# A ViT block on one core: order of VectorE's work in a step, order of SyncE's loads, and who stores the last rows

## Chip, cores and metric

The kernel runs on one core of one Trainium2 chip. The metric is the device time of one execution in microseconds, as the median of several runs. The engines are called PE (TensorE), PEld (its weight loads), ACT (ScalarE), DVE (VectorE), POOL (GpSimd) and SP (SyncE, which here only issues DMAs).

## What is computed

```python
# x (128,224,224,3) f32: an image and four cropped copies of it, in patches of 16x16
h = tokens(x) @ W + b                     # (128, 196, 192), W folded over the five copies
h = concat([cls_tok, h], axis=1)          # (128, 197, 192)
n = (h - mean(h)) / sqrt(var(h) + 1e-5)
q, k, v = n @ Wq.T, n @ Wk.T, n @ Wv.T    # 6 heads of 32
s = q k^T * 32**-0.5 + lam * anchor_sim   # per head
h = h + (softmax(s) @ v) @ Wo.T
n = layernorm(h)
i = clip(round(n / 0.02), -128, 127)      # int8
h = h + (i @ weight_t) * 0.0002 + bias
```

## The kernel before

There are two blocks of code, one after the other, each with a program for every engine, and a barrier between them.

**The token block** (`build_tokens`) holds all 128 images on the partitions and works through the 14 rows of 14 patches. DVE transposes pixels, PE multiplies by the folded weights, DVE adds the bias and takes the statistics (`bn_stats`), POOL forms the factors (`norm_factors`, nine small links, each waiting for the one before) and normalises. `h` and the normalised `xn` go to scratch tensors in HBM by POOL's DMA queue. Of the last row POOL normalises only the first `EARLY` = 8 of 14 tokens in this block and stores them (line 590). The other six follow in the next block: POOL forms their factors, DVE normalises them (line 1183), SP stores them (line 767). Meanwhile POOL sets a row of ones in `k_st` (line 1230), for which PE waits before its first image.

**The image block** (`build_attention`) is a software pipeline over the images. In step `i`, f = image i+5 is transposed (its `x_hi` and `x_lo` parts are made), pair p is projected to q and k, a = i+1 gets its scores and their maxima, b = i is scored again transposed and exponentiated (heads 0 to 4), c = i-1 is attended, e = i-2 gets output projection and h1, g = i-3 is normalised and quantised, k = i-4 goes through the last product and is stored. Steps alternate: in an odd step PE projects two blocks of a pair, in an even step the third. The first 12 images and the last 8 are written out, those between run in a loop of six steps. The order in each engine is written out by hand.

fp32 operands are split in a high part (made by ACT) and a low part (DVE: `x_lo`, `qk_lo`, `a_lo`), and PE multiplies the parts.

What matters here, engine by engine, in one step:
- PE: score 0 and 1; projection (line 803, it waits for `x_lo` of the step before); score_t 5 of c; in odd steps a second projection; score 2; last product; attend; score_t 0; score 3; output projection; score_t 1; turn back; transposes of `xn_in`; score 4; score_t 2; transposes of `qx` (wait for quantise); transposes of `att` (wait for DVE's product, line 1140); score 5; score_t 3; values; score_t 4; transposes of the maxima's parts.
- DVE: maxima 0 and 1; `qk_lo`; maximum 2; y; maximum 3; quantise of g (lines 1118 and 1121, waits for POOL); h1 of e (line 1129); reciprocal and `att` of c; maxima 4 and 5; the maxima's two parts (1150, 1152); `x_lo` of f (1160); `a_lo` of c (1168); statistics of e (1173).
- POOL: h1 plus bias (1198), wait for the statistics, nine links (139 to 147), `qx` (1216).
- SP: DMA issues for the q_st and k_st copies of a pair (707), the output (749, 750), the load of `xn_in` (714, 715: image i+6, two buffers), of `h_in` (756), and the maxima's rows into `q_st` (761).

Score h (h from 2) waits for maximum h-2, as two banks take turns.

Of the kernel before, what the change touches and what calls it, by code (L numbers as in the profile page):

```python
# [14 lines left out]
B, IMG, CH = 128, 224, 3  # L15
# [3 lines left out]
D = 192  # L19
# [130 lines left out]
def build_tokens(nc, s):  # L150
# [61 lines left out]
    h_stored = [sem(f"h_stored{i}") for i in range(2)]  # L212
    xn_stored = sem("xn_stored")

    SMALL = 16 * 5
# [53 lines left out]
    with nc.Block() as block:  # L269
        @block.sync  # L270
        def _(sp):
            def load(dst, src, landed):
                sp.dma_start(dst, src).then_inc(landed, 16)

            for g, landed in ((1, left_landed), (2, left_landed), (3, right_landed), (4, right_landed), (0, whole_landed)):
                load(w_of[g], s["tok_w"][:, RAW_ORDER.index(g)], landed)
            load_half_row(sp, 0, (0, 1), x_half[0])
            load(tok_bias[:], s["tok_b"].rearrange("(o n) -> o n", o=1).broadcast_to([B, D]), biases_landed)
            load_half_row(sp, 1, (0, 1), x_half[1])
            for i, w in enumerate(("wq", "wk", "wv")):  # L280
# [12 lines left out]

            rows(sp, step)
            sp.wait_ge(biases_landed, 32)

        @block.tensor
# [226 lines left out]
        def _(pool):  # L524
# [33 lines left out]
            def step(t):  # L558
# [28 lines left out]
                if first:  # L587
                    pool.dma_start(h_dram[:, 0, :], h_t[:, 0, G, :]).then_inc(cls_landed, 16)
                    pool.dma_start(xn_dram[:, 0, :], xn_t[:, G, :]).then_inc(xn_stored, 16)
                pool.dma_start(xn_dram[:, bass.ds(at_token, T), :] if last else xn_dram[:, bass.ds(at_token, G), :],  # L590
                               xn_t[:, 0:T if last else G, :]).then_inc(xn_stored, 16)

            rows(pool, step)

    return pads_stored, cls_landed, h_stored, xn_stored


def build_attention(nc, s):
# [7 lines left out]
    h_t, xn_t, stats, ln, o_bank = (s[n] for n in ("h_t", "xn_t", "stats", "ln", "o_bank"))  # L606
    pads_stored, cls_landed, h_stored, xn_stored = s["tokens_stored"]
    NS, NP = 2, 3
    MOD = 2 * NP
# [7 lines left out]
    def tile(name, shape, dt=F32):  # L617
        return sb(name, shape, dt, attention)

    xn_in = tile("xn_in", [TC, NS, 2, DA + 2 * DB])  # L620

# [81 lines left out]
    with nc.Block() as block:  # L703
        @block.sync
        def _(sp):
# [4 lines left out]
            def load_xn(n):  # L710
                if n.reuses(NS):
                    sp.wait_ge(xt_done, n.count(1, 1 - NS))
                by_chunk = xn_dram[n.n].rearrange("(c p) d -> p c d", p=TC)
                sp.dma_start(xn_in[:, n.two, :, 0:D], by_chunk).then_inc(xn_landed[n.slot], 16)
                sp.dma_start(xn_in[:, n.two, :, D:DA + 2 * DB], by_chunk[:, :, DA:D]).then_inc(xn_landed[n.slot], 16)

            def step(i):
                f, p, a, c, k, ahead = i.plus(5), pair_of(i), i.plus(1), i.plus(-1), i.plus(-4), i.plus(6)
                if i.fixed and i.n == -5:
                    load_xn(f)  # L720
                if p.within(B) and i.r % 2:
                    q_first, q_last, k_first = (0, 4), (4, H), (0, SPLIT)
# [24 lines left out]
                if k.within(B):  # L747
                    sp.wait_ge(y_done, k.count(1, 1))
                    sp.dma_start(out[k.n, 0:TC, :], y[:, k.two, 0, :]).then_inc(y_stored[k.slot], 16)
                    sp.dma_start(out[k.n, TC:NTOK, :], y[0:NTOK - TC, k.two, 1, :]).then_inc(y_stored[k.slot], 16)  # L750
                if ahead.within(B):
                    load_xn(ahead)
                if c.within(B):
# [17 lines left out]
            for p in range(2):  # L771
                sp.wait_ge(h_stored[p], 16 * (G // 2 - p))
            sp.wait_ge(xn_stored, 16 * (G + 1))
            images(sp, step)
# [4 lines left out]
        def _(pe):  # L779
            def turn(bank, src, n, width):  # L780

                for ic in range(2):
                    for c in range(2):
                        last = pe.transpose(bank[0:width, ic * TP + c * TC:ic * TP + (c + 1) * TC],  # L784
                                            src[:, n.two, c, ic * width:(ic + 1) * width], ident[0:TC, 0:TC])
                return last
# [90 lines left out]
            def step(i):  # L877
# [68 lines left out]
                if has_f:  # L946
# [7 lines left out]
                    turn(MISC[2], xn_in, f, DA).then_inc(xt_done, 1)  # L954
                if has_a:
# [3 lines left out]
                if has_g:  # L959
                    pe.wait_ge(quant_done, g.count(2, 2))  # L960
                    if has_e:
                        pe.wait_ge(h1_done, e.count(1, 1))
                    elif has_k:
                        pe.wait_ge(qxt_done, k.count(1, 1))
                    turn(MISC[0], qx, g, DC).then_inc(qt_done, 1)
                if has_c:

                    pe.wait_ge(norm_done, c.count(1, 1))
                    turn(o_bank[:, 0, :], att, c, DC).then_inc(at_done, 1)
                if has_a:  # L970
# [102 lines left out]
        def _(dve):  # L1073
# [15 lines left out]
            def step(i):  # L1089
# [15 lines left out]
                if has_k:  # L1105
                    dve.wait_ge(ff_done, k.count(1, 1))
                    dve.wait_ge(hb_done, k.count(1, 1))
                    if k.reuses(NS):
# [4 lines left out]
                        .then_inc(y_done, 1)  # L1113
                if has_a:
                    maxima(a, 3)
                if has_g:
# [4 lines left out]
                    nc.vector.tensor_scalar(qx[:, g.two, :, :], qx[:, g.two, :, :], MAGIC + 127.0, MAGIC - 128.0,  # L1121
                                            ALU.min, ALU.max).then_inc(quant_done, 1)
                if has_e:

# [18 lines left out]
                if has_a:  # L1143
# [4 lines left out]
                    if a.reuses(NS):  # L1148
# [4 lines left out]
                                            max_parts[:, a.two, :, 0:H].bitcast(F32),  # L1153
                                            ALU.subtract).then_inc(mpart_done, 1)
                if has_f:
                    dve.wait_ge(xhi_done, f.count(1, 1))
# [7 lines left out]
                if has_c:  # L1164
                    dve.wait_ge(ahi_done, c.count(1, 1))
                    if c.reuses(NS):
                        dve.wait_ge(op_done, c.count(1, 1 - NS))
                    nc.vector.tensor_tensor(a_lo[:, c.two, :, :], wide(o_bank[:, 0, :], DC),
                                            a_hi[:, c.two, :, :].bitcast(F32), ALU.subtract).then_inc(alo_done, 1)
                if has_e:  # L1170
                    dve.wait_ge(h1_done, e.count(1, 1))
                    for cc in range(2):
                        last = nc.vector.bn_stats(st2[:, e.two, cc, :], h1[:, e.two, cc, :])  # L1173
                    last.then_inc(st2_done, 1)

# [14 lines left out]
        def _(pool):  # L1190
# [32 lines left out]
            def link_last(ins):  # L1223
# [4 lines left out]
            norm_factors(nc, link_last, stats[:, LAST, EARLY:G, :], [ln[:, LAST, i, EARLY:G] for i in range(8)],  # L1228
                         minus_half[:, 0:G - EARLY])
            pool.memset(k_st[ST:ST + 2, :, :, :, :].bitcast(F32), 1.0).then_inc(ones_made, 1)  # L1230
            images(pool, step)
# [39 lines left out]
```

## Time and profile before

Three runs took 1878.80, 1881.69 and 1881.96 us, median 1881.69. The profiled execution took 1878.63 us, of which 1876.9 us are the span of the trace.

| | PE | PEld | DVE | ACT | POOL |
|---|---|---|---|---|---|
| busy us | 1752.2 | 1597.9 | 1413.3 | 781.9 | 740.3 |
| share of the span | 93% | 85% | 75% | 42% | 39% |

The token block lasts until 432 us, the pipeline of images is full from about 512 us. TensorE's granted clock is at its full level in all but the slices around the start of either block and the last one. Matmuls are pipelined, so the time that one takes is best read as the distance from its start to the start of the next.

### The profile page before, as it was taken

The numbers are of one execution on the slowest core, as the hardware profiler recorded it, in microseconds if no ns is written. First come the engines' busy times: TensorE is split into PE (matmuls) and PEld (weight loads), VectorE is DVE, ScalarE is ACT, GpSimd is POOL, SyncE is SP. The second block draws the span as 40 slices with busy tenths as digits, with TensorE's granted clock in tenths as the row PEclk, the third lists the DMA queues.
The fourth block names the chain that finished last, engine by engine and source line by source line (L and its number), as shares of the span: only waits on it lengthen the run. The fifth ranks groups of instructions, "written<-read, shape, count | busy, mean of one in ns | idle before, by whom it ended". The sixth has DMA issues, their size and how long they took to land.

```text
span 1876.9 us, 51604 instructions
## 1 busy us (share of the span) xinstructions
PE 1752.2 (93%) x15344; PEld 1597.9 (85%) x15344; DVE 1413.3 (75%) x3646; ACT 781.9 (42%) x1878; POOL 740.3 (39%) x1910
## 2 busy tenths in 40 slices
PE   1999999992799999999999999999999999999995
PEld 1999999992688888888888888888888888888884
DVE  4888888883477777777777777777777777777773
ACT  2000000000355555555555555555555555555552
POOL 3343453452044343443434434344343443434434
PEclk8999999996899999999999999999999999999997
DMA  9789999954777777787777777778777787777751
GB/s 281 215 277 303 310 316 280 310 211 108 112 129 137 140 134 134 129 134 139 134 135 128 134 139 134 135 128 134 139 134 135 128 133 138 135 136 127 135 99 30
DMA packets 214779, 303.57 MB, mean 162 GB/s; under 512 B 47584, under 2 KB 203635, under 8 KB 204612
## 3 DMA queue, kind: packets, MB, share of 16 engines
q1 hardware_dynamic: 204542, 227.27, 64.0%
q10 hardware_dynamic: 6054, 38.54, 7.2%
q0 software_dynamic: 4128, 37.06, 5.1%
q8 instruction: 30, 0.49, 0.1%
q14 instruction: 25, 0.20, 0.0%
HBM read 126.49 MB, written 58.29 MB: 98 GB/s over the span
## 4 chain that ended last, share of the span: by engine, by line
issue 30%; POOL 23%; PE 9%; DVE 8%; POOLq 3%; DMA 1%; SPq 1%; ACT 0%; DVEq 0%; ACTq 0%
POOL hb L1198 6%; POOL ln L146 4%; POOL qx L1216 4%; DVE h L1129 3%; DVE qx L1118 2%; PE o_bank L863 2%; PE bank L803 2%; POOLq L1208 2%; POOL ln L139 1%; POOL ln L145 1%; POOL ln L143 1%; POOL ln L147 1%; POOL ln L144 1%; POOL ln L141 1%; POOL ln L142 1%
## 5 line engine op out<-in xcount | busy, mean ns | idle before, releaser
L1078 DVE TENSOR_REDUCE neg_max<-bank 99x2 f32<-99x394 f32 x768 | 419.9, 560 | 243.7 <-PE bank L835 242.5
L1005 ACT ACTIVATE probs<-bank 99x396 f32<-99x396 f32 x768 | 383.5, 499 | 278.6 <-PE bank L847 278.4
L317 PE MATMUL bank<-e_t,xt 128*128 128x192 f32 x2352 | 388.3, 329 | 39.0 <-DVE xt L403 22.4
L317 PEld LDWEIGHTS bank<-e_t,xt 128*128 128x128 f32 x2352 | 386.8, 192 | 40.3 <-DVE xt L403 23.5
L847 PE MATMUL bank<-q_st,k_st 98*99 98x198 f32 x1536 | 284.5, 267 | 11.2 <-DMA q_st<-max_rows 6.1
L863 PE MATMUL o_bank<-probs,vals 99*64 99x198 f32 (+1 forms) x3072 | 290.3, 337 | 0.4 <-issue 0.3
L835 PE MATMUL bank<-k_st,q_st 96*99 96x198 f32 x1536 | 275.1, 274 | 7.5 <-issue 3.3
L863 PEld LDWEIGHTS o_bank<-probs,vals 99*64 99x64 f32 (+1 forms) x3072 | 213.0, 137 | 48.6 <-issue 1.1
L847 PEld LDWEIGHTS bank<-q_st,k_st 98*99 98x99 f32 x1536 | 202.5, 166 | 59.0 <-issue 36.5
L403 DVE STREAM_TRANSPOSE xt<-x_t 128x256 f32<-128x256 f32 x588 | 214.9, 416 | 44.7 <-PE bank L317 44.2
L999 ACT ACTIVATE x_hi<-bank 128x396 fp32r<-128x396 f32 x128 | 63.3, 495 | 414.2 <-PE bank L784 414.2
L1198 POOL TENSOR_TENSOR hb<-h,ffn_bias 99x384 f32<-99x384 f32 x128 | 128.3, 1003 | 244.8 <-DVE h L1129 244.8
L835 PEld LDWEIGHTS bank<-k_st,q_st 96*99 96x99 f32 x1536 | 192.5, 167 | 28.4 <-DVE neg_max L1078 13.9
L999 ACT ACTIVATE o_t<-o_bank 97x396 f32<-97x396 f32 (+1 forms) x256 | 93.1, 416 | 294.5 <-PE o_bank L863 294.5
L139 POOL TENSOR_TENSOR ln<-st 99x2 f32<-99x2 f32 x128 | 25.3, 198 | 405.7 <-DVE st L1173 405.7
L1216 POOL TENSOR_SCALAR qx<-h,ln 99x192 f32<-99x192 f32 x256 | 127.4, 505 | 41.0 <-POOL ln L147 41.0
L146 POOL TENSOR_TENSOR ln<-ln,minus_half 99x2 f32<-99x2 f32 (+2 forms) x143 | 127.5, 892 | 25.4 <-POOL ln L145 25.3
L1086 DVE TENSOR_TENSOR qk_lo<-bank,qk_hi 128x396 fp32r<-128x396 f32 x192 | 108.6, 565 | 30.8 <-ACT qk_hi L1012 27.0
L824 PE MATMUL bank<-wo_lo,a_hi 96*99 96x192 f32 x512 | 128.9, 252 | 0.0
L823 PE MATMUL bank<-wo_hi,a_hi 96*99 96x192 f32 x512 | 128.8, 252 | 0.0
L825 PE MATMUL bank<-wo_hi,a_lo 96*99 96x192 f32 x512 | 128.7, 251 | 0.0
L1012 ACT ACTIVATE qk_hi<-bank 128x396 fp32r<-128x396 f32 x192 | 96.3, 502 | 50.3 <-PE bank L803 42.3
(121 smaller groups left out, 3340.3 us busy)
## 6 DMA issues: line engine op xcount, KB each, us to landing
x_t<-in_x_dram ACTq DMA_DIRECT2D x26, 1344.0 KB, 18.3
x_t<-in_x_dram SPq DMA_DIRECT2D x26, 1344.0 KB, 22.1
q_st<-qk_hi SPq DMA_DIRECT2D x128, 198.0 KB, 4.2
k_st<-qk_hi SPq DMA_DIRECT2D x128, 198.0 KB, 4.7
xn_in<-xn_scratch SPq DMA_DIRECT2D x128, 148.5 KB
h_in<-h_scratch SPq DMA_DIRECT2D x128, 148.5 KB
h_scratch<-h_t POOLq DMA_DIRECT2D x13, 1344.0 KB, 17.6
xn_scratch<-xn_t POOLq DMA_DIRECT2D x13, 1344.0 KB, 8.2
```

Of the source, the lines that this page charges most:

```text
L146: link(nc.gpsimd.tensor_tensor(v[6], v[4], half, ALU.pow))
L317: last = pe.matmul(token_bank(p)[:, 0:D], xt[:, p, c // 3, c % 3, :], e_t[:, row_kind(t), col, c // 3, c % 3, :], start=c == 0, stop=c == 5)
L403: last = nc.vector.transpose(xt[:, p, :, c, :].rearrange("p m (g b) -> p g m b", b=32), pix[:, c])
L824: pe.matmul(acc, hi, wo_lo[:, ic, :], start=False, stop=False)
L835: last = pe.matmul(S_BANK[h % 2][0:TC, c * TP:(c + 1) * TP], q_st[0:ST, n.pair, h, n.two, c * TC:(c + 1) * TC], k_st[0:ST, n.pair, h, n.tw ...
L847: last = pe.matmul(T_BANK[0:TC, c * TP:(c + 1) * TP], k_st[:, n.pair, h, n.two, c * TC:(c + 1) * TC], q_st[:, n.pair, h, n.two, :], start= ...
L863: last = pe.matmul(o_bank[half * TW:(half + 1) * TW, p // 2, (p % 2) * TP:(p % 2 + 1) * TP], vals[0:kk, n.two, kc, h, :], probs[0:kk, n.tw ...
L999: nc.scalar.activation(dst, src, ACT.Copy, **affine).then_inc(done, 1)
L1005: nc.scalar.activation(probs[:, n.two, h, :, :], wide(T_BANK, TC), ACT.Exp).then_inc(exp_done, 1)
L1078: nc.vector.tensor_reduce(out=neg_max[:, n.two, :, h], in_=wide(S_BANK[h % 2], TC)[:, :, 0:NTOK], axis=AX_X, op=ALU.max, negate=True).then ...
L1198: nc.gpsimd.tensor_tensor(hb[:, e.two, :, :], h1[:, e.two, :, :], ffn_bias[:].unsqueeze(1).broadcast_to([TC, 2, D]), ALU.add).then_inc(hb_ ...
L1216: nc.gpsimd.tensor_scalar(qx[:, e.two, cc, :], h1[:, e.two, cc, :], v[7][:, cc:cc + 1], v[6][:, cc:cc + 1], ALU.add, ALU.mult).then_inc(ln ...
```

## The change

- SP stores the first eight tokens of the last row, behind a wait for POOL's normalisation, with a semaphore of its own; POOL no longer does.
- POOL's memset of ones in `k_st` waits for DVE's six normalisations.
- `xn_in` has three buffers instead of two. SP loads image i+7 at the head of its step, ahead of the copies of q and k; before, it was image i+6, behind the output.
- DVE quantises g before maximum 3 and not behind it.
- DVE takes the statistics of e right behind the maxima's parts, and then `x_lo` and `a_lo`.

```diff
+            at_token = (G - 1) * G + 1                      # SP, end of the token block
+            sp.wait_ge(ln_step, G * LN_PER)
+            sp.dma_start(xn_dram[:, at_token:at_token + EARLY, :], xn_t[:, 0:EARLY, :]).then_inc(early_stored, 16)
...
-                pool.dma_start(xn_dram[:, bass.ds(at_token, T), :] if last else xn_dram[:, bass.ds(at_token, G), :],
-                               xn_t[:, 0:T if last else G, :]).then_inc(xn_stored, 16)
+                if not last:
+                    pool.dma_start(xn_dram[:, bass.ds(at_token, G), :], xn_t[:, 0:G, :]).then_inc(xn_stored, 16)
...
-    xn_in = tile("xn_in", [TC, NS, 2, DA + 2 * DB])
+    xn_in = tile("xn_in", [TC, NX, 2, DA + 2 * DB])         # NX = 3
...
-                if n.reuses(NS):
-                    sp.wait_ge(xt_done, n.count(1, 1 - NS))
+                if n.reuses(NX):
+                    sp.wait_ge(xt_done, n.count(1, 1 - NX))
...
-                f, p, a, c, k, ahead = i.plus(5), pair_of(i), i.plus(1), i.plus(-1), i.plus(-4), i.plus(6)
+                f, p, a, c, k, ahead = i.plus(5), pair_of(i), i.plus(1), i.plus(-1), i.plus(-4), i.plus(7)
                 if i.fixed and i.n == -5:
                     load_xn(f)
+                    load_xn(f.plus(1))
+                if ahead.within(B):
+                    load_xn(ahead)
...
-                if ahead.within(B):                         # behind the output's stores
-                    load_xn(ahead)
...
-            sp.wait_ge(xn_stored, 16 * (G + 1))
+            sp.wait_ge(xn_stored, 16 * G)
+            sp.wait_ge(early_stored, 16)
...
-                if has_a:                                   # DVE
-                    maxima(a, 3)
                 if has_g:
                     dve.wait_ge(ln2_step, g.count(LN2_PER, LN2_PER))
...
+                if has_a:
+                    maxima(a, 3)
                 if has_e:
...
+                if has_e:                                   # DVE, behind the maxima's parts
+                    dve.wait_ge(h1_done, e.count(1, 1))
+                    for cc in range(2):
+                        last = nc.vector.bn_stats(st2[:, e.two, cc, :], h1[:, e.two, cc, :])
+                    last.then_inc(st2_done, 1)
                 if has_f:                                   # x_lo; then a_lo
...
-                if has_e:                                   # the same four lines, behind a_lo
...
+            pool.wait_ge(last_row_xn, G - EARLY)
             pool.memset(k_st[ST:ST + 2, :, :, :, :].bitcast(F32), 1.0).then_inc(ones_made, 1)
```

## Rows read from the trace of the kernel before

**Rows 1.** Waits: engine, line, tile, releaser; us in total, times, longest.
```profile
POOL ln L139 <- DVE st L1173: 405.7, 127, 3.3
SPq L761 <- ACT max_rows L999: 325.4, 123, 8.0
```
**Rows 2.** Time line of PE in the loop: start us, us, engine, line, operands, count.
```profile
1003.01 0.35 PE L847 MATMUL bank<-q_st,k_st 98*99 98x198 f32 x2
...
1004.21 0.38 PE L784 MATMUL o_bank<-ident,att 99*96 99x99 f32 x2 [0.22 <-DVE att L1140]
...
1014.42 0.35 PE L847 MATMUL bank<-q_st,k_st 98*99 98x198 f32 x2
...
1014.97 0.38 PE L784 MATMUL o_bank<-ident,att 99*96 99x99 f32 x2
...
1018.59 0.34 PE L803 MATMUL bank<-x_lo,wb_rest 97*128 97x396 f32 x1
1018.87 0.34 PE L835 MATMUL bank<-k_st,q_st 96*99 96x198 f32 x1
...
1024.49 0.35 PE L847 MATMUL bank<-q_st,k_st 98*99 98x198 f32 x2
...
1025.53 0.38 PE L784 MATMUL o_bank<-ident,att 99*96 99x99 f32 x2
```
**Rows 3.** Time line of DVE in the same steps.
```profile
1005.96 0.63 DVE L1160 TENSOR_TENSOR x_lo<-bank,x_hi 128x198 fp32r<-128x198 f32 x2
...
1016.72 0.63 DVE L1160 TENSOR_TENSOR x_lo<-bank,x_hi 128x198 fp32r<-128x198 f32 x2
...
1017.74 0.60 DVE L1173 BATCH_NORM_STATS2 st<-h 99x6 f32<-99x192 f32 x2
1018.27 0.54 DVE L1078 TENSOR_REDUCE neg_max<-bank 99x2 f32<-99x394 f32 x1
...
1023.52 0.36 DVE L1118 TENSOR_SCALAR qx<-qx 99x384 f32<-99x384 f32 x1 [0.57 <-POOL qx L1216]
...
1024.19 0.55 DVE L1129 TENSOR_TENSOR h<-bank,h_in 99x384 f32<-99x384 f32 x1
...
1059.25 0.63 DVE L1160 TENSOR_TENSOR x_lo<-bank,x_hi 128x198 fp32r<-128x198 f32 x2
```
**Rows 4.** Time line of PE's weight loads, first load of a projection.
```profile
1006.70 0.19 PEld L803 LDWEIGHTS bank<-x_hi,wa_hi 128*128 128x128 f32 x1
...
1017.75 0.19 PEld L803 LDWEIGHTS bank<-x_hi,wa_hi 128*128 128x128 f32 x1
...
1060.42 0.19 PEld L803 LDWEIGHTS bank<-x_hi,wa_hi 128*128 128x128 f32 x1
```
**Rows 5.** Chain that ended last, image block's start: start us, us, what.
```profile
449.48 0.91 PE bank L784 x4
...
483.49 0.53 SPq L714
...
484.54 4.43 DMA q_st<-max_rows
```
**Rows 6.** Drains of lines 269 and 703 (ends of blocks): ns min/median/max, first/last start.
```profile
L269 POOLq DRAIN  x1: 5038/5038/5038, 427.1 to 427.1; - x1
L269 DVEq DRAIN  x1: 399/399/399, 427.8 to 427.8; - x1
...
L703 POOLq DRAIN  x1: 1074/1074/1074, 1869.6 to 1869.6; - x1
```
**Rows 7.** Lines 1183 and 1230: ns min/median/max, first and last start us.
```profile
L1183 DVE TENSOR_SCALAR xn_t<-h_t,ln x6: 360/364/6173, 436.1 to 443.4; 128x192 f32<-128x192 f32 x6
...
L1230 POOL MEMSET k_st<- x1: 6032/6032/6032, 436.1 to 436.1; 2x7128 f32 x1
```
**Rows 8.** Time line of DVE near the end.
```profile
1855.25 0.56 DVE L1140 TENSOR_TENSOR att<-o_bank,inv_sum 99x384 f32<-99x384 f32 x1
...
1857.46 0.61 DVE L1173 BATCH_NORM_STATS2 st<-h 99x6 f32<-99x192 f32 x2
```

More of the change, by code:

```diff
@@ L213, in build_tokens @@
     xn_stored = sem("xn_stored")
+    early_stored = sem("early_stored")
     SMALL = 16 * 5
@@ L589, in step @@
                     pool.dma_start(xn_dram[:, 0, :], xn_t[:, G, :]).then_inc(xn_stored, 16)
-                pool.dma_start(xn_dram[:, bass.ds(at_token, T), :] if last else xn_dram[:, bass.ds(at_token, G), :],
-                               xn_t[:, 0:T if last else G, :]).then_inc(xn_stored, 16)
+                if not last:
+                    pool.dma_start(xn_dram[:, bass.ds(at_token, G), :], xn_t[:, 0:G, :]).then_inc(xn_stored, 16)
             rows(pool, step)
-    return pads_stored, cls_landed, h_stored, xn_stored
+    return pads_stored, cls_landed, h_stored, xn_stored, early_stored
 def build_attention(nc, s):
@@ L606, in build_attention @@
     h_t, xn_t, stats, ln, o_bank = (s[n] for n in ("h_t", "xn_t", "stats", "ln", "o_bank"))
-    pads_stored, cls_landed, h_stored, xn_stored = s["tokens_stored"]
-    NS, NP = 2, 3
+    pads_stored, cls_landed, h_stored, xn_stored, early_stored = s["tokens_stored"]
+    NS, NP, NX = 2, 3, 3
     MOD = 2 * NP
@@ L710, in load_xn @@
             def load_xn(n):
-                if n.reuses(NS):
-                    sp.wait_ge(xt_done, n.count(1, 1 - NS))
+                if n.reuses(NX):
+                    sp.wait_ge(xt_done, n.count(1, 1 - NX))
                 by_chunk = xn_dram[n.n].rearrange("(c p) d -> p c d", p=TC)
-                sp.dma_start(xn_in[:, n.two, :, 0:D], by_chunk).then_inc(xn_landed[n.slot], 16)
-                sp.dma_start(xn_in[:, n.two, :, D:DA + 2 * DB], by_chunk[:, :, DA:D]).then_inc(xn_landed[n.slot], 16)
+                sp.dma_start(xn_in[:, n.slot % NX, :, 0:D], by_chunk).then_inc(xn_landed[n.slot], 16)
+                sp.dma_start(xn_in[:, n.slot % NX, :, D:DA + 2 * DB], by_chunk[:, :, DA:D]).then_inc(xn_landed[n.slot], 16)
             def step(i):
-                f, p, a, c, k, ahead = i.plus(5), pair_of(i), i.plus(1), i.plus(-1), i.plus(-4), i.plus(6)
+                f, p, a, c, k, ahead = i.plus(5), pair_of(i), i.plus(1), i.plus(-1), i.plus(-4), i.plus(7)
                 if i.fixed and i.n == -5:
                     load_xn(f)
+                    load_xn(f.plus(1))
+                if ahead.within(B):
+                    load_xn(ahead)
                 if p.within(B) and i.r % 2:
@@ L779, in _, with turn @@
         def _(pe):
-            def turn(bank, src, n, width):
+            def turn(bank, src, at, width):
                 for ic in range(2):
@@ L784, in turn @@
                         last = pe.transpose(bank[0:width, ic * TP + c * TC:ic * TP + (c + 1) * TC],
-                                            src[:, n.two, c, ic * width:(ic + 1) * width], ident[0:TC, 0:TC])
+                                            src[:, at, c, ic * width:(ic + 1) * width], ident[0:TC, 0:TC])
                 return last
@@ L953, in step @@
                         pe.wait_ge(xlo_done, f.count(1, 0))
-                    turn(MISC[2], xn_in, f, DA).then_inc(xt_done, 1)
+                    turn(MISC[2], xn_in, f.slot % NX, DA).then_inc(xt_done, 1)
                 if has_a:
@@ L964, in step @@
                         pe.wait_ge(qxt_done, k.count(1, 1))
-                    turn(MISC[0], qx, g, DC).then_inc(qt_done, 1)
+                    turn(MISC[0], qx, g.two, DC).then_inc(qt_done, 1)
                 if has_c:
                     pe.wait_ge(norm_done, c.count(1, 1))
-                    turn(o_bank[:, 0, :], att, c, DC).then_inc(at_done, 1)
+                    turn(o_bank[:, 0, :], att, c.two, DC).then_inc(at_done, 1)
                 if has_a:
@@ L1169, in step @@
                                             a_hi[:, c.two, :, :].bitcast(F32), ALU.subtract).then_inc(alo_done, 1)
-                if has_e:
[L1171 to L1174, printed above, removed]
             nc.vector.memset(vals[:], 0.0).then_inc(consts, 1)
```

## The prediction

> **What bounds the kernel now.** I read the page of the profile first. TensorE (PE) is busy 93% of the span and VectorE (DVE) 75%, so the time is near a PE floor, and a DVE edit pays only where PE waits. Next the waits, sorted by total: GpSimd (POOL) stood 405.7 us for the statistics in 127 images, and SyncE (SP) 325.4 us for the maxima's rows [rows 1]. POOL is no bottleneck, so its wait costs nothing by itself; the question is who waits for what POOL makes. For that I read PE's own time line in the image loop. From the last product of score_t(b,2) to the transposes of `att` PE takes 0.55 us in an odd step (1014.42 to 1014.97), 1.04 in an even one (1024.49 to 1025.53) and 1.20 in every third even one (1003.01 to 1004.21), where the loop also jumps [rows 2]. So PE loses 0.49, 0.49 and 0.65 us in three pairs of images, 0.54 on average. DVE's time line says why: `quantise` began at 1023.52, released by POOL's qx, and h1, the reciprocal and `att` queue behind it [rows 3].
>
> This is a closed chain: statistics, POOL's nine links and qx, quantise, h1, att, PE's transposes, score 5, maxima 4 and 5, their parts, x_lo, a_lo, statistics again. It sets the pace of every step, so shortening it pays until PE's next wait.
>
> That next wait is the thing to look for. The weight load of the block projection (line 803) began at 1006.70, and x_lo, which it waits for, ran from 1005.96 for 0.63 us, to 1006.59: a hand-over of 0.11 us, hence already released by x_lo [rows 3, 4]. In an even step x_lo ended at 1017.35 and the load began at 1017.75, 0.40 later; in every third at 1059.88 and 1060.42, 0.54 later [rows 3, 4].
>
> **Part 1, statistics ahead of x_lo and a_lo.** In the old order x_lo began at 1016.72 and the statistics at 1017.74: they start 1.02 us sooner. The statistics occupy DVE for 0.53 us (1017.74 to 1018.27) [rows 3], and x_lo and a_lo come that much later. What it gives: POOL's qx is ready at 1022.50 instead of 1023.52. What it costs:
> - odd step: nothing covers x_lo, so the projection starts 0.53 us later.
> - even step: the cover is 0.40-0.11 = 0.29, so 0.24 is left; in every third 0.54-0.11 = 0.43, so 0.10.
> - given back: after the even projection, score 2 began 0.28 after the last product (1018.59 to 1018.87) because maximum 0 had begun only at 1018.27; its weight load is 0.19 long and sets the usual distance [rows 2 to 4]. A projection that starts later hides these 0.09, except in the third pair.
> a_lo is read only by the next step's attention, several us on: nothing, and if that cover were gone at most another 0.53.
>
> **Part 2, quantise ahead of maximum 3.** Quantise takes 0.67 (1023.52 to 1024.19), a maximum 0.48-0.57. New quantise: 1022.50 to 1023.17, then maximum 3 to 1023.65, then h1, 0.54 before its old 1024.19. PE's loss there was 0.49, so the whole loss goes, with 0.05 us in hand and 0.15 to 0.24 more from PE's own later projection. In odd steps the scores come 0.5 later too and quantise falls into DVE's idle time. Maximum 3 is later by up to 0.9 us, but only score 5 needs it, which comes after the transposes of `att`. The average per pair:
> two pairs of three: +0.53 +0.24 -0.09 -0.49 = +0.19; the third: +0.53 +0.10 -0.65 = -0.02; mean +0.12 us.
> 128 images are 64 pairs, less two at either end where the pipeline fills and empties: 60 such pairs, **+7.2 us**. The bounds: +0.02 a pair if the even delays were all hidden (0.53 against 0.54: 0 us), +0.24 if no score 2 wait is given back and 0.05 of the loss stays (14 us). I take 7.2, since each term is a start-to-start difference in a pattern that repeats to 0.02 us.
>
> **Part 3, token loads first in SP's step, third buffer.** The two loads take 1.05 us (483.49 to 484.54) [rows 5]. They stand before the maxima's rows in the same step and now fall into the time that SP spends waiting, 325.4 us in 123 steps, 2.6 a step [rows 1]. In the loop this is worth nothing: no PE wait there is on these loads. If that cover went, the q_st and k_st copies behind them would be up to 1.05 later, and they are used two steps on. At the start it is on the chain: PE waits for the first rows, issued at 484.54 and 4.43 us under way [rows 5]. They go out 1.05 sooner: **-1.0 us** (0 to -1.5). The third buffer lets image 3's load go early, but the first scores wait for the k_st copies, not for it: 0.
>
> **Part 4, the first stored rows by SP.** POOL's drain at the block's end lasted 5.04 us from 427.1, right behind its last store, to 432.2; DVE's ended at 427.8+0.4 = 428.2. At the kernel's end POOL's drain, with no store before it, took 1.07 us [rows 6]. So the drain waits for the store. With POOL's last store a whole row of tokens earlier, the barrier falls to DVE's end, 428.3: **-3.9 us**; were POOL's drain 5 us in any case, it would only start one store issue sooner, -0.6.
>
> **Part 5, POOL's ones behind the last rows.** Six normalisations of the last rows: 0.36 us each, but one took 6.17, and in exactly that time POOL's memset ran for 6.03, both from 436.1; the last began at 443.4, so the others follow at 0.3 [rows 7]. With the memset behind them the six take 5x0.29+0.36 = 1.8 instead of 7.6, and the rows are stored 5.8 us sooner. PE's first transposes, 449.48 before [rows 5], have them at 449.48-5.8 = 443.7. But now the memset starts at 436.1+1.8 = 437.9 and ends at 443.95, and PE waits for the ones: 444.05. So **-5.4 us** (from -6, if the memset overlaps all, to -4.2, if DVE's two memsets of x_lo, 1.2 us, had to queue behind it). I take the -5.4, since DVE's operations of the loop keep their 0.55 to 0.63 us beside POOL's links [rows 3], so it is not every operation that is shut out. The Trainium skill (SBUF — State Buffer, Who interferes with whom) says that GpSimd and a VectorE operation in a two-port mode exclude each other for the whole instruction; the trace agrees, 6.17 us against 0.36. By its rule DVE's memsets, with no SBUF input, would not queue either, and the term stays what it is.
>
> **The tail.** For the last image but one, the statistics stood behind a_lo, which waited for ScalarE: 1857.46, with `att` begun at 1855.25 and 0.56 long [rows 8]. They now follow `att`, some 0.5 behind its start: 1855.75, **-1.7 us** on the chain that ends the kernel. In the few steps just before there is no x_lo left: half a microsecond of a_lo leaves the chain and maximum 3 enters it with as much: 0.
>
> **Sum:** +7.2 -1.0 -3.9 -5.4 -1.7 = -4.8 us. Against the profiled execution, 1878.63 (span 1876.9), this gives 1873.8. That execution lies at the low end of the three runs (1878.80, 1881.69, 1881.96), so beside the median 1881.69 it is **1876.9 us**. The forecast's own range: steady part 0 to +14, barrier -0.6 to -3.9, ones -4.2 to -6, rows 0 to -1.5: 1869 to 1884.
>
> **Rivals.**
> - A: PE is not held by x_lo. Then the 0.54 a pair comes in full: 60x0.54 = 32 us and the 12 us of start and tail: 1837. For it: POOL's chain is the longest loop now. Against it: the 0.11 us hand-over of rows 3 and 4. Chance 0.08.
> - B, slower: quantise holds DVE for POOL and maximum 3 then stands in front of h1. It decides as soon as maximum 3 ends after 1023.70, that is, if qx is ready later than 1022.55. If the old loss stays whole, the pair costs 0.53+0.13 = 0.66 more, 60x0.66 = 40, less 12: 1909. For it: only 0.05 us in hand. Against: PE's scores are themselves later, which leaves 0.2. Chance 0.07.
> - C: the change does not do what it says at the start: the barrier stays with POOL, so -0.6 instead of -3.9, and the sum is -1.5: 1880. Against: the 1.07 us drain. Chance 0.13.
> - D, slower by a little: the steady part at its upper bound and the gains of the start at their lower ones: +14 -0.6 -4.2 -1.7 = +7.5: 1889. For it: the even steps' terms are small differences, and each 0.1 us a pair is 6 us. Chance 0.10.
> The forecast has 0.62.
>
> **How the numbers follow.** Range 1868 to 1887: it leaves out A, B and a part of D, some 0.2. What tells a change from none is 0.2%, 3.8 us: 1877.9 to 1885.5. Faster: A 0.08, some two thirds of the forecast's 0.62 (its value is only 1 us inside the bound), 0.03 of C: 0.51. Slower: B 0.07, most of D 0.07, 0.04 of the rest: 0.18. Same: 0.31.
>
> **What would show it.** Right: the load of line 803 in odd steps still 0.11 us behind x_lo, with the statistics ahead of it; score_t to `att` 0.55 us in every step; three steady pairs 0.3 to 0.4 us longer than before (one is 1004.21 to 1025.53 = 21.32 [rows 2]); no 5 us drain and the second block starting near 428.3; the six normalisations at 0.36 each; PE's first transposes near 440.1. Wrong: pairs near 20.8 (A) or 22 (B), a drain of 5 us (C), or DVE's memsets 6 us long.

## The result and the profile after

Four runs of the changed kernel took 1859.11 to 1861.66 us, median **1860.83 us**. Four runs of the kernel before beside them took 1878.28 to 1881.96, median 1880.24: ratio **0.9898 (0.9883 to 0.9912)**. The profiled execution took 1860.42 us, span 1858.7, against 1876.9 before: -18.2. The sum of the prediction was -4.8, beside the median 1876.9 us with a range of 1868 to 1887: the measured time lies below the range. The direction was right, the size was not. One run of one experiment (e9) took 2405.72 us at a mean granted clock of 0.67, where every other run here had 0.97 to 0.98, and is left out of e9's ratio.

To see where the time went, the span is divided at two starts of h1 (the DVE operation of line 1129 before, 1135 after), the first and the 121st, which the trace gives to 0.01 us. The 120 steps between them are 60 pairs, the steady part:

| | first h1 | 121st h1 | between, per pair | 121st h1 to the end |
|---|---|---|---|---|
| before | 512.50 | 1792.07 | 21.33 | 84.8 |
| changed | 501.60 | 1775.61 | 21.23 | 83.1 |
| difference | **-10.9** | | -0.09, in 60 pairs **-5.6** | **-1.7** |

The start and the tail were forecast at -10.3 (-3.9 -5.4 -1.0) and -1.7. The steady part was forecast at +7.2 and is -5.6: of the 13.4 us between forecast and measured span, 12.8 are here.

The token block, which is the same in both up to its last stores, ends at nearly the same time in these two profiles. POOL's last normalisations start at 422.62 before and 422.67 changed:

```profile
422.62 3.90 POOL L582 TENSOR_SCALAR xn_t<-h_t,ln 128x192 f32<-128x192 f32 x8 [0.31 <-POOL ln L147]
...
422.67 3.89 POOL L586 TENSOR_SCALAR xn_t<-h_t,ln 128x192 f32<-128x192 f32 x8 [0.31 <-POOL ln L147]
```

In other profiles this start lies between 421.13 (e1) and 423.82 (e9), and no edit reaches back before it. So a first h1 is compared by its distance from this start where tenths of a microsecond matter: 89.88 before, 78.93 changed.

The chain that ended last, from the page of the kernel before:

```profile
issue 30%; POOL 23%; PE 9%; DVE 8%; POOLq 3%; DMA 1%; SPq 1%; ACT 0%; DVEq 0%; ACTq 0%
```

and the page of the changed kernel, busy times and the same chain:

```profile
PE 1737.3 (93%) x15344; PEld 1602.8 (86%) x15344; DVE 1409.2 (76%) x3646; ACT 781.9 (42%) x1878; POOL 738.7 (40%) x1909
...
PE 62%; DVE 7%; issue 3%; POOL 2%; ACT 1%; SPq 1%; DMA 1%; DVEq 0%; POOLq 0%
```

PE now stands for 62% of the chain (9% before) and POOL for 2% (23%). So the chain no longer goes round through POOL's links. The waits of the changed kernel say the same (columns as in [rows 1]):

```profile
SPq L766 <- ACT max_rows L1005: 396.5, 127, 7.0
...
POOL ln L139 <- DVE st L1164: 277.4, 127, 2.3
...
DVE qx L1122 <- POOL qx L1222: 124.3, 128, 3.0
...
PE bank L809 <- DVE x_lo L1171: 25.7, 63, 1.3
```

POOL waits 277.4 us for the statistics and not 405.7 [rows 1]. And 63 projections of PE, one in each odd step, have `x_lo` named as what ended their wait; before, only two had. This is the next wait that the prediction looked for. The time line of PE (columns as in [rows 2]) has first the projection of an even step, then that of an odd one, then that of every third even step, and last the transposes of `att` in every third even step:

```profile
1002.92 0.41 PE L841 MATMUL bank<-k_st,q_st 96*99 96x198 f32 x2
...
1005.55 0.42 PE L809 MATMUL bank<-x_hi,wa_hi 128*128 128x396 f32 x1
...
1012.08 0.35 PE L853 MATMUL bank<-q_st,k_st 98*99 98x198 f32 x2
...
1012.62 0.55 PE L790 MATMUL o_bank<-ident,att 99*96 99x99 f32 x4
1012.95 0.41 PE L841 MATMUL bank<-k_st,q_st 96*99 96x198 f32 x2
...
1015.58 0.42 PE L809 MATMUL bank<-x_hi,wa_hi 128*128 128x396 f32 x1 [0.41 <-DVE x_lo L1171]
...
1045.29 0.41 PE L841 MATMUL bank<-k_st,q_st 96*99 96x198 f32 x2
...
1048.01 0.36 PE L809 MATMUL bank<-x_hi,wa_hi 128*128 128x396 f32 x1
...
1054.49 0.35 PE L853 MATMUL bank<-q_st,k_st 98*99 98x198 f32 x2
...
1055.13 0.55 PE L790 MATMUL o_bank<-ident,att 99*96 99x99 f32 x4
```

From score_t(b,2) to the transposes of `att` PE now takes 0.54 us in this even step (1012.08 to 1012.62), as in odd steps before [rows 2]: the loss of 0.49 is gone. In every third even step it takes 0.64 (1054.49 to 1055.13), so 0.10 of that loss stays. From score 5 to the projection it takes 2.63 in the even and the odd step (1002.92 to 1005.55, 1012.95 to 1015.58) and 2.72 in every third even one (1045.29 to 1048.01). The same two starts in the kernel before, odd step, even step and every third even one:

```profile
1004.54 0.41 PE L835 MATMUL bank<-k_st,q_st 96*99 96x198 f32 x2
...
1006.74 0.43 PE L803 MATMUL bank<-x_hi,wa_hi 128*128 128x396 f32 x1
...
1015.29 0.41 PE L835 MATMUL bank<-k_st,q_st 96*99 96x198 f32 x2
...
1017.84 0.36 PE L803 MATMUL bank<-x_hi,wa_hi 128*128 128x396 f32 x1
...
1057.83 0.41 PE L835 MATMUL bank<-k_st,q_st 96*99 96x198 f32 x2
...
1060.51 0.36 PE L803 MATMUL bank<-x_hi,wa_hi 128*128 128x396 f32 x1
```

That is 2.20, 2.55 and 2.68. So the projection is late by 0.43 in the odd step (forecast 0.53), by 0.08 in the even one (0.24) and by 0.04 in every third (0.10). DVE's time line shows why, changed kernel, from the second of the maxima's parts on:

```profile
1014.21 0.17 DVE L1158 TENSOR_TENSOR max_parts<-neg_max,max_parts 99x12 fp32r<-99x12 f32 x1
1014.29 0.61 DVE L1164 BATCH_NORM_STATS2 st<-h 99x6 f32<-99x192 f32 x2
1014.82 0.61 DVE L1171 TENSOR_TENSOR x_lo<-bank,x_hi 128x198 fp32r<-128x198 f32 x2
```

and of the kernel before, the last two of the same operations:

```profile
1005.79 0.17 DVE L1152 TENSOR_TENSOR max_parts<-neg_max,max_parts 99x12 fp32r<-99x12 f32 x1
1005.96 0.63 DVE L1160 TENSOR_TENSOR x_lo<-bank,x_hi 128x198 fp32r<-128x198 f32 x2
```

The statistics do occupy DVE for 0.53 (1014.29 to 1014.82). But they start 0.08 us after the parts' subtraction (1014.21), where `x_lo` used to start 0.17 after it (1005.79 to 1005.96). So `x_lo` now starts 0.61 behind that subtraction instead of 0.17: 0.44 later and not 0.53. It also ends in 0.61 instead of 0.63, so the odd step's projection is 0.42 to 0.43 later. PE's product follows `x_lo`'s end at 0.15 in both kernels (1006.59 to 1006.74, 1015.43 to 1015.58).

The even step's cover was also larger than I reckoned. A weight load of the changed kernel (columns as in [rows 4]):

```profile
1015.55 0.19 PEld L809 LDWEIGHTS bank<-x_hi,wa_hi 128*128 128x128 f32 x1 [0.55 <-issue]
```

In the even step before, the product came 0.09 behind its load (1017.75 to 1017.84); a held PE starts it 0.03 behind (1015.55 to 1015.58). The cover has to be taken from product to product: 1017.84 less `x_lo`'s end 1017.35 less 0.15 is 0.34 and not 0.29. So 0.42 less 0.34 leaves the 0.08 measured. In every third even step `x_lo` ends at 1047.77 and the product starts at 1048.01, 0.24 behind it and not 0.15: there `x_lo` does not hold PE.

Now the start. POOL's drain at the end of the token block (columns as in [rows 6]):

```profile
L270 POOLq DRAIN  x1: 2605/2605/2605, 426.7 to 426.7; - x1
```

the last rows' normalisation and the ones (as in [rows 7]):

```profile
L1189 DVE TENSOR_SCALAR xn_t<-h_t,ln x6: 373/374/379, 433.2 to 434.7; 128x192 f32<-128x192 f32 x6
...
L1237 POOL MEMSET k_st<- x1: 6032/6032/6032, 435.2 to 435.2; 2x7128 f32 x1
```

and the chain from there (as in [rows 5]):

```profile
435.18 6.04 POOL k_st L1237
441.31 0.91 PE bank L790 x4
...
474.53 0.60 SPq L711
475.18 3.56 DMA q_st<-max_rows
```

POOL's drain is 2.6 us and no longer 5.0, so it ends at 429.3 (before 432.1). The six normalisations take 0.37 each; none is 6 us long. PE's first transposes begin at 441.31 (449.48), and the first maxima's rows go out at 475.18 (484.54) and land in 3.56 us (4.43) [rows 5]. In the tail, DVE's time line of the changed kernel (as in [rows 8]) has the statistics right behind `att`:

```profile
1838.89 0.56 DVE L1146 TENSOR_TENSOR att<-o_bank,inv_sum 99x384 f32<-99x384 f32 x1
1839.37 0.61 DVE L1164 BATCH_NORM_STATS2 st<-h 99x6 f32<-99x192 f32 x2
```

They start 0.48 behind it, against 2.21 before [rows 8]: 1.73 us sooner. The granted clock of TensorE also differs between the two tails, with no edit for it: in the three stretches of 12 us from 48 us before the end on, it is 0.92, 0.79 and 0.78 before, 1.00, 0.84 and 0.50 in the changed kernel (1.00 is 2.4 GHz, 0.50 is 1.2 GHz, and a value between is the mean of a stretch that has both).

### The profile page after: what moved, and what is told of

The parts are those of the page before. It is cut to its first block, busy times and chain, and to the rows that moved or that the text cites. A ratio compares the mean times of both kernels' runs of the same rounds, so it can differ in the third digit from the quotient of the medians.

```text
span 1858.7 us, 51623 instructions
## 1 busy us (share of the span) xinstructions
PE 1737.3 (93%) x15344; PEld 1602.8 (86%) x15344; DVE 1409.2 (76%) x3646; ACT 781.9 (42%) x1878; POOL 738.7 (40%) x1909
## 4 chain that ended last, share of the span: by engine, by line
PE 62%; DVE 7%; issue 3%; POOL 2%; ACT 1%; SPq 1%; DMA 1%; DVEq 0%; POOLq 0%
PE o_bank L869 14%; PE bank L809 10%; PE bank L853 8%; PE bank L841 6%; PE bank L790 5%; PE o_bank L879 3%; PE bank L818 3%; PE o_bank L790 3%; PE bank L829 2%; PE bank L830 2%; PE bank L831 2%; PE bank L924 2%; DVE neg_max L1084 2%; DVE x_lo L1171 2%; ACT probs L1011 1%
## 5 line engine op out<-in xcount | busy, mean ns | idle before, releaser
L841 PE MATMUL bank<-k_st,q_st 96*99 96x198 f32 x1536 | 271.0, 272 | 14.6 <-DMA k_st<-qk_lo 9.7
L1122 DVE TENSOR_SCALAR qx<-qx 99x384 f32<-99x384 f32 x128 | 46.1, 360 | 124.3 <-POOL qx L1222 124.3
L146 POOL TENSOR_TENSOR ln<-ln,minus_half 99x2 f32<-99x2 f32 (+2 forms) x143 | 127.4, 891 | 25.4 <-POOL ln L145 25.3
L139 POOL TENSOR_TENSOR ln<-st 99x2 f32<-99x2 f32 x128 | 25.2, 197 | 277.4 <-DVE st L1164 277.4
```

Of the source, the lines that this page charges most:

```text
L841: last = pe.matmul(S_BANK[h % 2][0:TC, c * TP:(c + 1) * TP], q_st[0:ST, n.pair, h, n.two, c * TC:(c + 1) * TC], k_st[0:ST, n.pair, h, n.tw ...
```

## The experiments

The theory was that the statistics' new place frees POOL's chain and hands the pace to `x_lo`, at the sizes just read. Its rivals: the loads' new place or third buffer gives the steady gain; or it is quantise's place that frees PE. Each experiment is a part of the change on the kernel before, or one or two moves on the changed one; in the diffs a comment stands for the lines of an operation that is moved whole, and `...` for lines left out.

**e1, both edits on DVE alone** (before, with the statistics and quantise as in the change):

```diff
-    maxima(a, 3)
     # quantise g
+    maxima(a, 3)
...
     # maxima's parts of a
+    # bn_stats of e
     # x_lo of f; a_lo of c
-    # bn_stats of e
```

> The kernel before with both edits of DVE's order (statistics right behind the maxima's parts, quantise ahead of maximum 3) and nothing else. Theory 1 (a ring of DVE and POOL set the pace; now PE waits for x_lo instead): pairs of 21.24 us on average, 0.1 below before, so 60 x 0.1 = 6 us, and 1.7 us of the tail: -8 us, near 1872. Theory 2 (the steady gain comes from the token loads at the head of SP's step): pairs as my sum had them, 0.12 longer, and about +5 us.

Measured: 1870.54 us, ratio 0.9955 (0.9942 to 0.9967). Pairs of 21.23 us. All of the steady gain is here, without loads, store or ones. The loads are not its cause. The first h1 is at 510.40, 2.1 sooner, but 1.5 of that is the token block's earlier end in this profile: from POOL's last normalisations (421.13) it is 89.27 us, 0.6 less than before.

**e2, the statistics' place alone:**

```diff
     # maxima's parts of a
+    # bn_stats of e
     # x_lo of f; a_lo of c
-    # bn_stats of e
```

> The kernel before with the statistics behind the maxima's parts, quantise left behind maximum 3. Theory 1: qx is ready 1.0 us sooner, maximum 3 still fits in front of quantise without delaying h1, so the steady pairs are those of both edits (21.24), and the tail steps gain some tenths more: -8 to -9 us. Theory 3 (quantise ahead of maximum 3 is what frees PE): PE's loss before att stays and the later x_lo is paid on top: pairs of 21.8, +25 us.

Measured: 1869.80 us, 0.9951 (0.9937 to 0.9966); pairs 21.23, tail 82.1 us (e1: 83.2). The same as e1 within the intervals, so quantise's place adds nothing to it.

**e3, quantise's place alone:**

```diff
-    maxima(a, 3)
     # quantise g
+    maxima(a, 3)
```

> The kernel before with quantise ahead of maximum 3, statistics left behind a_lo. Theory 1: maximum 3 (0.48 us) enters the ring statistics-POOL-quantise-h1-att-score 5, which takes 10.65 us a step: 11.1 a step, 22.2 a pair, 60 x 0.9 = +50 us or so, near 1930. Theory 3: this edit alone shortens the pairs, -5 us or more.

Measured: 1929.20 us, 1.0267 (1.0252 to 1.0282): 49 us slower, pairs of 22.08. Waits of this kernel:

```profile
DVE qx L1116 <- POOL qx L1216: 293.6, 128, 4.4
```

DVE stands 293.6 us in front of quantise (52.5 before), with maximum 3 and h1 queued behind it. From score_t(b,2) to the transposes of `att` PE takes some 1.5 us in even steps (1.04 before) and 0.84 in odd ones (0.55). This is rival B's mechanism: with the statistics still late, moving quantise forward costs 0.75 us a pair.

**e4, only the start** (SP's early store, and POOL's ones behind the normalisations; POOL's own issue of that store goes, as in the change, and is left out here):

```diff
+            sp.wait_ge(ln_step, G * LN_PER)
+            sp.dma_start(xn_dram[:, at_token:at_token + EARLY, :], xn_t[:, 0:EARLY, :]).then_inc(early_stored, 16)
...
+            pool.wait_ge(last_row_xn, G - EARLY)
             pool.memset(k_st[ST:ST + 2, :, :, :, :].bitcast(F32), 1.0).then_inc(ones_made, 1)
```

> The kernel before with SP storing the first eight tokens of the last row and POOL's memset behind the six normalisations; no edit in the image loop. From the trace of the changed kernel: the barrier 2.9 us sooner, PE's first transposes 8.2 us sooner, pairs unchanged at 21.34: -8 us, near 1872. If the copies' landing that follows absorbs some of it, less.

Measured: 1875.36 us over 11 runs (1870.03 to 1877.23), 0.9971 (0.9961 to 0.9982). In its profile the first h1 is at 504.79, 7.7 us sooner, and pairs are the old 21.33; but from the 121st h1 to the end it takes 89.7 instead of 84.8 us. So 4.9 of the 7.7 us are given back in the tail, and the expected 1872 was missed. The granted clock fell with it. Windows of e4 in its last 50 us (stretch, us, busy us and count of PE, PEld, DVE, ACT, POOL, granted clock, DMA share, GB/s):

```profile
1832.20:1838.20 6.00, 6.00 (x37) 5.26 (x34) 1.27 (x3) 1.33 (x4) 2.09 (x5) 0.50 0.18 51
1838.20:1844.20 6.00, 4.82 (x25) 3.78 (x23) 1.89 (x6) 3.06 (x7) 1.59 (x4) 0.50 0.00 0
```

and of the kernel before at about the same distance from its end:

```profile
1834.90:1840.90 6.00, 4.83 (x40) 4.11 (x40) 2.60 (x8) 2.72 (x7) 2.04 (x8) 0.85 0.09 25
1840.90:1846.90 6.00, 5.48 (x46) 4.39 (x43) 2.07 (x5) 2.46 (x6) 2.22 (x5) 0.87 0.10 27
```

PE ran at 0.50 of its clock (1.2 GHz) throughout in e4, at a mean of 0.85 and 0.87 before, with fewer matmuls in the same time. From the 125th to the 127th h1 it took 25.2 us against 21.3. What tips it is not known; nothing in e4's edits touches the tail. Its eleven runs lie in two groups (four at 1870.0 to 1873.2, seven at 1875.2 to 1877.2), a distance that fits this loss, and the mean granted clock of the run is 0.976 to 0.977 in each of the four and 0.971 to 0.972 in each of the seven. Only one of them, of the second group, has a trace.

**e5, the loads alone** (first in SP's step, third buffer):

```diff
-    NS, NP = 2, 3
+    NS, NP, NX = 2, 3, 3
...
+                if ahead.within(B):            # ahead = i.plus(7)
+                    load_xn(ahead)
                 # copies of q_st and k_st, output
-                if ahead.within(B):            # ahead = i.plus(6)
-                    load_xn(ahead)
```

> The kernel before with the third buffer and the token loads at the head of SP's step, and nothing else. Theory 1: worth nothing in the loop (pairs 21.33 as before); at the start the first maxima's rows go out 1.0 us sooner and land a bit sooner: first h1 near 511, -1 to -2 us in all, near 1878. Theory 2 (the loads brought the steady gain): pairs of 21.24 or less, -7 us.

Measured: 1877.78 us over 12 runs, 0.9987 (0.9978 to 0.9996). Pairs are unchanged at 21.33, the first h1 is at 510.39 instead of 512.50: 2.1 us sooner (1.9 from the last normalisations), where I forecast 1.0. The theory that the loads gave the steady gain falls. The chain of e5's start, last issue of a copy and the rows:

```profile
482.31 0.60 SPq L707
482.95 3.44 DMA q_st<-max_rows
```

The rows leave at 482.95, not 484.54: 1.6 us sooner, where the two loads account for 1.05, and they land in 3.44 us instead of 4.43 [rows 5]. The same rows take 3.36 to 3.56 us in the changed kernel and in e6 to e9, and 4.32 to 4.50 in e1 to e4, e10 and e11, which have the loads in the old place. So the quicker landing comes with the loads' new place; why is not shown. The forecast counted only the 1.05.

**e6, statistics between `x_lo` and `a_lo`, quantise back behind maximum 3** (from the changed kernel). If the theory is right, `x_lo` keeps its old place behind the parts, the statistics still come half a microsecond sooner, and neither chain holds PE:

```diff
+    maxima(a, 3)
     # quantise g
-    maxima(a, 3)
...
-    # bn_stats of e
     # x_lo of f
+    # bn_stats of e
     # a_lo of c
```

> The changed kernel, but DVE's order at the end of a step is x_lo, statistics, a_lo, and quantise stands behind maximum 3 as before. Theory 1: x_lo is as early as before, so PE's odd steps lose the 0.43 us again that it now waits; the statistics are 0.5 us earlier than before, which gives qx at about 1023.04 in the old times of rows 3, quantise done by 1023.7, just in time for h1: PE's wait before att nearly gone, pairs of 20.8 us, 25 us below the changed kernel, near 1835. If x_lo is not what holds PE: pairs of 21.2 as in the changed kernel, 1860.

Measured: **1834.51 us**, ratio 0.9760 (0.9746 to 0.9775). Pairs of 20.84 us. DVE's time line of this kernel:

```profile
1004.40 0.17 DVE L1158 TENSOR_TENSOR max_parts<-neg_max,max_parts 99x12 fp32r<-99x12 f32 x1
1004.57 0.63 DVE L1166 TENSOR_TENSOR x_lo<-bank,x_hi 128x198 fp32r<-128x198 f32 x2
1005.12 0.60 DVE L1173 BATCH_NORM_STATS2 st<-h 99x6 f32<-99x192 f32 x2
```

and PE's, score 5 and the projection of the next step:

```profile
1003.14 0.41 PE L841 MATMUL bank<-k_st,q_st 96*99 96x198 f32 x2
...
1005.34 0.42 PE L809 MATMUL bank<-x_hi,wa_hi 128*128 128x396 f32 x1
```

`x_lo` follows the subtraction at 0.17 again, the projection follows score 5 at 2.20 as in the odd step before, and the wait for POOL hardly comes back: PE takes 0.55 us from score_t(b,2) to the transposes of `att`, 0.72 in every third even step. Against before, 60 pairs of 0.49 us less are 29.1 us, the start 10.9 and the tail (78.6 for 84.8) 6.2: together the 46.3 us between 1876.9 and this kernel's span of 1830.6. The 6.2 are not the order's alone: from 48 to 24 us before the end the granted clock is 1.00 here, where it was 0.92 and 0.79 before. It is the best version here, 26 us ahead of the changed kernel.

**e7, e6 with quantise left in front of maximum 3** (changed kernel, statistics moved only):

```diff
-    # bn_stats of e
     # x_lo of f
+    # bn_stats of e
     # a_lo of c
```

> As the kernel with the order x_lo, statistics, a_lo, but quantise stays ahead of maximum 3. Theory 1: the ring is 10.1 us with maximum 3 in it plus 0.55 for x_lo, 10.65 a step: pairs of 21.3 as before, so only the start and the tail gain: 1865 to 1868. Theory 3 (the place of quantise does not matter once the statistics are early): as its sister, near 1835.

Measured: 1865.45 us, 0.9919 (0.9905 to 0.9933); its profiled run, at 1869.12, is the longest of the four, with a tail of 86.5 us at a granted clock of 0.50 in its last 36 us. Pairs of 21.33. Its DVE time line:

```profile
1011.78 0.36 DVE L1122 TENSOR_SCALAR qx<-qx 99x384 f32<-99x384 f32 x1 [2.03 <-POOL qx L1222]
...
1012.46 0.56 DVE L1084 TENSOR_REDUCE neg_max<-bank 99x2 f32<-99x394 f32 x1
1012.93 0.55 DVE L1135 TENSOR_TENSOR h<-bank,h_in 99x384 f32<-99x384 f32 x1
```

DVE stands idle for 2.03 us in front of quantise with maximum 3 queued behind it, and h1 comes last of the three. The order of two operations is worth 0.49 us a pair, 31 us in all (1865.45 - 1834.51), and in favour of the old order; 29 of the 31 are in the loop.

**e8, the changed kernel with POOL waiting for its own stores before the drain:**

```diff
             rows(pool, step)
+            pool.wait_ge(xn_stored, 16 * G)
```

> The changed kernel with one more wait: at the end of the token block POOL waits until its own stores of normalised rows have landed. If POOL's drain (2.6 us in the changed kernel, 5.0 before) waits for stores under way, the drain behind this wait is short, under 0.5 us, and the barrier stays near 429.3. If the drain has a cost of its own, it stays at 2 us or more and the barrier comes later than 429.3. Time 1860 either way, within 3 us.

One run: 1860.41 us, first h1 501.43. Its drain, behind that wait:

```profile
L270 POOLq DRAIN  x1: 2607/2607/2607, 426.3 to 426.3; - x1
```

All of POOL's own stores of normalised rows had landed, and the drain took 2.6 us all the same. The edit adds no waiting: the kernel already waits for the same count before its last normalisations, so the new wait is met when POOL reaches it, and the drain begins 0.3 us behind the normalisations' end. POOL's last store of `h` was issued at 401.7, and no store of `h` took more than 20.3 us to land, so it had landed too. These 2.6 us are not a wait for POOL's stores, here or in the changed kernel.

**e9, the changed kernel with quantise back behind maximum 3:**

```diff
+    maxima(a, 3)
     # quantise g
-    maxima(a, 3)
```

> The changed kernel with quantise back behind maximum 3, statistics still ahead of x_lo. Theory 1: PE is held by x_lo, and qx is ready with room for either order, so the pairs stay at 21.24 and the time at 1859 to 1861; the edit of quantise is worth nothing here. Theory 3: PE waits for quantise again, pairs of 21.7, 1890.

Measured: 1859.84 us as the median of four, 0.9894 (0.9876 to 0.9912), pairs 21.23. Three of its runs lie at 1858.70 to 1860.02; the fourth is the one of 2405.72 us, and what lowered its clock is not known. In the changed kernel quantise's place is worth nothing. e6 differs from this kernel by the statistics' place alone, and is 25.3 us faster.

**e10, only the ones behind the normalisations, and e11, only the store by SP** (e4 taken apart; the rest of e11's edit is left out, as in e4):

```diff
+            pool.wait_ge(last_row_xn, G - EARLY)      # e10 alone
...
+            sp.dma_start(xn_dram[:, at_token:at_token + EARLY, :], xn_t[:, 0:EARLY, :]).then_inc(early_stored, 16)   # e11 alone
```

> The kernel before with POOL's memset of the ones behind the six normalisations, and nothing else: the six take 1.8 us instead of 7.6, PE's first transposes 5.3 us sooner; -5 us if the later chain keeps it, near 1875. The tail can differ by some us with the step in which TensorE's clock falls.

> The kernel before with SP storing the first eight tokens of the last row, and nothing else: POOL's drain 2.6 us instead of 5.0, barrier 2.9 us sooner, -3 us, near 1877. The forecast had -3.9, as it took the drain to be nothing without the store.

Measured: e10 1874.60 us over 9 runs, 0.9976 (0.9966 to 0.9986), first h1 5.3 us sooner (4.9 from the last normalisations). Its profiled run, at 1878.44, is the longest of the nine and has a tail as long as e4's (89.8 us); the others lie at 1873.6 to 1876.0. e11 1871.92 us, 0.9963 (0.9950 to 0.9977), first h1 2.9 us sooner (3.4 from the last normalisations) and tail 1.0 shorter; the rest of its gain, 3.1 us, lies in the loop. So e11 missed its expectation of 1877 by 5 us. In its loop three pairs took 21.36, 21.25 and 21.25 us, where before, e4 and e10 have 21.39, 21.26 and 21.36, and no instruction of the loop differs. The difference lies in PE's wait before `att` in even steps: 1.01, 1.02 and 1.09 us from score_t(b,2), where before it is 1.03, 1.04 and 1.22. The loop can thus run in two patterns, 0.15 us in three pairs apart. What chooses between them stays open. It also bounds how finely a change in the loop can be read here: the steady gain of 5.6 us is shown because every profile with the statistics ahead of `x_lo` has 21.23 (changed, e1, e2, e8, e9), and every profile with the old DVE order 21.27 (e11) or 21.33 (before, e4, e5, e10).

## Why the prediction was wrong

**The chain, right.** Statistics, POOL, quantise, h1, att, PE was the chain that set the pace, and `x_lo` to the projection was the next wait. e2 shows the first, e6 the second: with both nearly out of the way the pair falls by 0.49.

**Part 1, statistics ahead of `x_lo`: this step failed, by its sizes.** The text had +0.12 a pair on average, "+7.2 us"; the steady part is -5.6. Its four terms, and what PE's time lines of the two kernels give for them as means over the loop (16 times three pairs each; us per pair):

| | odd projection | even projection | given back | PE's loss before `att` | sum |
|---|---|---|---|---|---|
| two pairs of three, forecast | +0.53 | +0.24 | -0.09 | -0.49 | +0.19 |
| measured | +0.43 | +0.09 | -0.12 | -0.49 | -0.09 |
| every third pair, forecast | +0.53 | +0.10 | 0 | -0.65 | -0.02 |
| measured | +0.43 | +0.04 | -0.04 | -0.57 | -0.14 |

The mean of the measured terms is -0.11 a pair (-0.10 with unrounded terms), and the pairs themselves say -0.09 over all 60 and -0.10 over these. So nothing of size is left unexplained. The cost of the later projections is what was mis-sized: the odd ones by 0.10 (6 us in 60 pairs), the even ones by 0.12 on average (7 us). The wait that is given back was 0.03 larger (2 us), and every third pair kept 0.10 us of the loss that was to go whole (the other way, 2 us). Together that is about the 13 us between +7.2 and -5.6.

The reason for the odd term: an operation that moves does not carry the length that it had elsewhere. 0.53 is right for the statistics' own stretch, but the stretch between the subtraction and its follower shrank from 0.17 to 0.08, and `x_lo` from 0.63 to 0.61. For the even terms the cover was 0.34 and not 0.29, taken from product to product. The forecast said that each term was exact to 0.02 us; this pair of neighbours was never in the trace of before. The lowest bound was wrong too: "+0.02 a pair" stands for 0.53 against 0.54, which is -0.01. Of the signs named, three steady pairs were to be 0.3 to 0.4 us longer; they are 0.3 shorter.

**Part 2, quantise ahead of maximum 3: wrong in its reason.** I let it remove the loss of 0.49. e2 and e9 show that the statistics alone do that (0.55 us from score_t(b,2) to `att` in both, 0.64 in every third even step). e3 and e7 show what it can do instead: 49 us slower than before and 31 us slower than e6, where the statistics are late. In the changed kernel it is neutral because they are early enough. Rival B thus had its mechanism right, and in the changed kernel its point of decision was not reached.

**Part 3, loads: -1.0 forecast, -1.9 to -2.1 measured** (e5). The edit also let the rows land sooner, 3.44 us and not 4.43. Under-sized.

**Part 4, barrier: -3.9 forecast, -2.9 measured** (the drain's end moves 432.1 to 429.3; the first h1 of e11 comes 2.9 sooner, 3.4 from the last normalisations). The text's "So the drain waits for the store" holds for 2.4 of its 5.0 us. The 1.07 us drain at the kernel's end [rows 6] was the wrong row to reckon the rest by: this one costs 2.6 with no store of POOL under way (e8). Over-sized, and rival C, a drain still of 5 us, fell.

**Part 5, ones: -5.4 forecast, -5.3 measured** (e10; at the first h1, from the last normalisations, 4.9 of it are left). Right, with its mechanism: the normalisations take 0.37 each, and the memset holds PE. PE's transposes come 0.1 behind the memset's end (441.22 to 441.31), as reckoned. DVE's two memsets of `x_lo` ran beside POOL's from 435.23 on in 1.18 us and did not queue. The Trainium skill (SBUF — State Buffer, Who interferes with whom), that GpSimd and a two-port VectorE operation shut each other out, had the trace with it before, 6.17 us against 0.36 [rows 7], and has it now: with the memset moved away, the operation is 0.37 long.

**The tail: -1.7 forecast, -1.7 measured.** The statistics come 1.73 us sooner, as reckoned. But the two tails ran at different granted clocks, and e2, with the statistics alone, has a tail 2.7 shorter, where e1 has 1.6 and e9, with quantise in its old place, 3.1. So the agreement of the two numbers is in part luck.

In sum: counted from POOL's last normalisations, the start's parts measured alone are -1.9 (e5), -3.4 (e11) and -4.9 (e10), together -10.2, and DVE's new order adds some tenths (0.2 in e2, 0.6 in e1), for which the forecast had no term; all together it is -10.9. That the forecast's -10.3 comes so near is luck: loads and barrier erred in opposite directions. The steady part was -5.6 for +7.2.

## To carry to other kernels

A queue with two rings is sped up by moving the one that sets the pace only as far as leaves the other alone: here, with quantise in its old place, the whole move ran in 1859.8 us (e9) and half of it, to between `x_lo` and `a_lo`, in 1834.5 (e6). When an operation goes between two neighbours, take its cost as the shift of the start behind it, and allow a tenth of a microsecond for gaps whose pair of neighbours the trace has not shown; in 120 steps that is 12 us, which decided the sign here. An operation that waits for another engine goes behind whatever does not depend on it, unless what it waits for is surely there.

## What the runs showed of the hardware that I had not expected

- The gap after a small operation depends on the one that follows: behind the 0.17 us subtraction the statistics start 0.08 later, `x_lo` 0.17 later (1004.40 to 1004.57 in e6 too). The statistics read and write SBUF, `x_lo` reads PSUM and has two waits in front of it where the statistics have one; whether either is the reason was not tried.
- POOL's drain at the end of the token block takes 2605 to 2607 ns with no store of its own under way (changed, e8), 5038 right behind a store [rows 6], and the one at the kernel's end 1074 (1066 in the changed kernel). What it does in the 2.6 us stays open.
- While the pipeline runs empty the same stretch can have a granted clock of 0.50 or of 0.85 (e4 and before). In the profiles of e3, e4, e7 and e10 it took 24.8 to 25.2 us from the 125th to the 127th h1, in all others 18.1 to 21.3. In e4 and e10 this gave back 5 us of what was gained 1300 us earlier, and no edit of theirs touches the tail.
- The first maxima's rows land in 3.36 to 3.56 us where the token loads are not issued just before them (changed, e5 to e9), and in 4.32 to 4.50 where they are (before, e1 to e4, e10, e11). Why is not shown.
